# First batch of the first attention convolved, projected and split one learning step earlier; values cleared first

## Time and profile before

| | us |
|---|---|
| median of three runs | 3385.29 (3382.37 to 3389.59) |
| the profiled execution | 3388.66 |
| its span | 3386.8 |

### The profile page before, as it was taken

The page is one execution under the profiler, slowest core; times in us unless marked ns, Lnnn a source line. Parts: engine busy times, 40 slices in busy tenths (PEclk is TensorE's granted clock), DMA queues, the critical chain, the costliest instruction groups (busy, mean ns, idle before and its releaser), DMA issues. The chain is left out here.

```text
span 3386.8 us, 83147 instructions
## 1 busy us (share of the span) xinstructions
PE 3115.7 (92%) x33099; PEld 1852.8 (55%) x33099; DVE 2534.1 (75%) x5014; ACT 2057.6 (61%) x4153; POOL 877.2 (26%) x783
## 2 busy tenths in 40 slices
PE   6887799999999999999999999789999999999997
PEld 5776322222223677777777777545555554555554
DVE  5777788888887476677667766677887877778874
ACT  6775288888888443333434334247777666776776
POOL 3322311111111322342233224224342211111110
PEclk9998799999999999999999999889999999999999
DMA  4100122222221110010001101223333232222222
GB/s 142 36 20 4 54 80 83 78 81 84 81 75 53 34 30 30 23 33 29 29 23 33 35 23 30 49 77 95 90 93 81 79 98 86 80 78 80 84 61 67
DMA packets 234976, 204.91 MB, mean 61 GB/s; under 512 B 74340, under 2 KB 190852, under 8 KB 234500
## 3 DMA queue, kind: packets, MB, share of 16 engines
q1 hardware_dynamic: 228484, 195.50, 20.1%
q0 software_dynamic: 6144, 4.72, 1.0%
HBM read 73.61 MB, written 59.39 MB: 39 GB/s over the span
## 5 line engine op out<-in xcount | busy, mean ns | idle before, releaser
L1624 DVE TENSOR_REDUCE b_maxima<-psum 128x2 f32<-128x1024 f32 (+3 forms) x768 | 779.8, 1041 | 227.0 <-PE psum L1421 216.9
L1565 ACT ACTIVATE b_prob<-psum 128x512 f32<-128x512 f32 (+2 forms) x1536 | 725.5, 526 | 298.4 <-PE psum L1454 292.0
L1624 DVE TENSOR_REDUCE c_maxima<-psum 128x2 f32<-128x1024 f32 x512 | 592.5, 1213 | 58.1 <-PE psum L1415 57.3
L1565 ACT ACTIVATE c_prob<-psum 128x512 f32<-128x512 f32 x1024 | 547.2, 600 | 113.9 <-PE psum L1447 97.3
L2378 PEld LDWEIGHTS psum<-consts_layer,a_hid 128*128 128x128 f32 x4096 | 477.5, 192 | 53.8 <-issue 53.6
L2368 PE MATMUL psum<-a_x1t,consts_layer 128*128 128x512 f32 x1024 | 462.1, 595 | 20.8 <-ACT a_hid L2438 13.8
L2378 PE MATMUL psum<-consts_layer,a_hid 128*128 128x128 f32 x4096 | 479.0, 275 | 0.0
L2438 ACT ACTIVATE a_hid<-psum,consts_layer 128x512 f32<-128x512 f32 x512 | 347.0, 687 | 197.2 <-PE psum L2368 190.5
L1478 PE MATMUL psum<-b_prob,b_v 128*32 128x128 f32 (+3 forms) x5632 | 398.4, 371 | 15.9 <-ACT b_c L1572 15.4
L1447 PE MATMUL psum<-b_qa,b_ka 64*128 64x512 bf16 (+3 forms) x2048 | 344.2, 303 | 40.1 <-ACT b_prob L1565 26.0
L2605 DVE SCALAR_TENSOR_TENSOR a_acc<-psum,a_gprob,a_acc 128x128 f32<-128x128 f32 x512 | 143.7, 343 | 261.1 <-PE psum L2378 233.1
(11 more groups left out here) (407 smaller groups left out, 4200.7 us busy)
## 6 DMA issues: line engine op xcount, KB each, us to landing
b_qa<-b_part SPq DMA_DIRECT2D x192, 128.0 KB
b_context<-b_c SPq DMA_DIRECT2D x64, 256.0 KB, 2.1
c_qa<-c_part SPq DMA_DIRECT2D x96, 128.0 KB, 2.5
c_ka<-c_part SPq DMA_DIRECT2D x96, 128.0 KB, 2.6
b_ka<-b_part SPq DMA_DIRECT2D x96, 128.0 KB
c_context<-c_c SPq DMA_DIRECT2D x32, 256.0 KB, 2.1
b_scale<-b_inverse SPq DMA_DIRECT2D x64, 128.0 KB
b_unscaled<-b_context SPq DMA_DIRECT2D x64, 128.0 KB
```

Source lines behind the costliest of these rows:

```text
L1565: self.nc.scalar.activation(out, src, ACT.Exp, scale=SCALE).then_inc(self.s.free, 1)
L1624: self.nc.vector.reduce_max(out, src, X).then_inc(self.m.free, 1)
```

## The change

- The convolution of batch 0 and its copies move from step 6 (`NC - 2`) to step 5 (`NC - 3`), behind the norm; it waits for the last silu of chunk 7. `transpose_k(7)` waits for its copies.
- The projection and its copies move from step 7 to step 6, behind `transpose_k(7)` and a wait for both copies of `kt`.
- The four operations of the splits move from GpSimd in step 7 to VectorE: three ahead of the update of step 6 (`vector_parts`), the last at the start of step 7 (`vector_last`).
- GpSimd clears `qa` and `ka` at the start of step 6 and not behind its roots.
- In the setup of the first attention, the values' buffer is cleared before the row of ones is set.

```diff
-    def pool_parts(self, pool, rest):
+    def vector_parts(self, dve, rest):
         nc, qk, part = self.nc, self.qk, self.part
-        pool.wait_ge(self.qk_copied, 2)
-        nc.gpsimd.tensor_copy(part[0][:, :, :], qk[:, :, :]).then_inc(self.parted, 1)
...
+        dve.wait_ge(self.qk_copied, 2)
+        nc.vector.tensor_copy(part[0][:, :, :], qk[:, :, :]).then_inc(self.parted, 1)
+        dve.wait_ge(self.parted, 1)
+        nc.vector.tensor_tensor(rest, qk[:, :, :], part[0][:, :, :], ALU.subtract).then_inc(self.parted, 1)
+        dve.wait_ge(self.parted, 2)
+        nc.vector.tensor_copy(part[1][:, :, :], rest).then_inc(self.parted, 1)
+
+    def vector_last(self, dve, rest):
+        dve.wait_ge(self.parted, 3)
+        self.nc.vector.tensor_tensor(self.part[2][:, :, :], rest, self.part[1][:, :, :], ALU.subtract).then_inc(self.parted, 1)
...
@@ learn, tensor: transpose_k(n)
+                    if n == NC - 1:
+                        pe.wait_ge(head.xc_copied, 2)
@@ learn, tensor, step s
-                    if s == NC - 1:
+                    if s == NC - 2:
+                        pe.wait_ge(kt_copied.sem, kt_copied.at(NC - 1, 2))
                         head.tensor_projection(pe)
...
                     norm(s)
-                    if s == NC - 2:
-                        pe.wait_ge(kt_copied.sem, kt_copied.at(NC - 1, 2))
+                    if s == NC - 3:
+                        pe.wait_ge(silu_ready.sem, silu_ready.at(NC - 1, 4))
                         head.tensor_convolution(pe)
@@ learn, gpsimd, step s
                     pool.wait_ge(mem_ready.sem, mem_ready.at(s, 0))
+                    if s == NC - 2:
+                        pool.wait_ge(proj_ready.sem, proj_ready.at(NC - 1, 4))
+                        pool.wait_ge(prod_ready.sem, prod_ready.at(NC - 1, 1))
+                        pool.wait_ge(xt_stored.sem, xt_stored.at(NC, 0))
+                        head.pool_clear()
...
                         output_deviations(s, h)
-                    if s == NC - 2:
-                        pool.wait_ge(proj_ready.sem, proj_ready.at(NC - 1, 4))
-                        pool.wait_ge(prod_ready.sem, prod_ready.at(NC - 1, 1))
-                        pool.wait_ge(xt_stored.sem, xt_stored.at(NC, 0))
-                        head.pool_clear()
-                    if s == NC - 1:
-                        pool.wait_ge(kn_ready.sem, kn_ready.at(NC - 1, 1))
-                        head.pool_parts(pool, tk[:, :, :].rearrange("p (k t) d -> p k (t d)", k=2))
@@ learn, vector, step s
+                    if s == NC - 1:
+                        head.vector_last(dve, rest)
                     for h in range(2):
                         hidden(s, h)
...
+                    rest = tk[:, :, :].rearrange("p (k t) d -> p k (t d)", k=2)
+                    if s == NC - 2:
+                        head.vector_parts(dve, rest)
                     update(s)
@@ Attention.pool_setup
         nc = self.nc
+        if self.done:
+            self.pool_value(pool, 0)
         nc.gpsimd.memset(self.one[:, :], 1.0).then_inc(self.tables_ready, 1)
...
-        self.pool_value(pool, 0)
+        if not self.done:
+            self.pool_value(pool, 0)
```

## The result

The changed kernel takes 3391.07 us (median of 18 runs, 3385.84 to 3399.01); the kernel before, timed beside it, takes 3385.47 (18 runs, 3381.62 to 3390.71). The ratio is 1.0017, 95% interval 1.001 to 1.0025: 5.6 us slower, where 3382.3 was forecast. The profiled execution took 3389.57 us (span 3387.8) against 3388.66 (span 3386.8) before.

A forecast was written before the change was run, and what follows sets the result against it. No engine is full in a learning step, so it is a chain of waits. -3.7 - 1.8 + 2.5 = -3.0 us, applied to the median 3385.29, gave 3382.3 us; range 3377.0 to 3388.5, chance 0.82.

The forecast's parts named there:

- Added: three VectorE operations ...: 0: Before step 6's update: three moved splits, 2.7 us, fit in VectorE's 3.18 us idle wait, costing 0.
- the fourth operation's 0: Ahead of step 7's hidden part: the last split, 1.23 us, fits in VectorE's 2.03 us idle wait, costing 0.
- any stretch behind 360 us changes its length by more than 1 us: Behind the learning stage: a stated sign that the forecast is wrong.
- Step 7's gradient part, -3.7: First squaring of y to next root: without GpSimd's splits it takes 25.95 us instead of 29.67.
- Step 6's hidden part, -1.8: Root to first squaring of y: moved convolution keeps TensorE's clock high, second tanh at 280.1 instead of 282.01.
- Rival B: Step 6's clock fall was chance, so the filler saves nothing: -0.5, 3384.8 us; 0.15 together with D.
- D: Step 7: VectorE's chain did not set the step, another wait takes over: about -0.5; 0.15 together with Rival B.
- Step 7's hidden part, +2.5: Root to first squaring of y: without the filler TensorE's clock falls, 13.70 us instead of 11.17.
- The projection, 0: Step 6: the moved products and key copies fit in free time, copies ending 0.4 us before along_y: 0.
- bound of +1.5: Step 6's projection: most it could cost if its second product ended 1.9 us later at the lower clock.
- Values' clearing, 0: First attention's setup: earlier clearing frees VectorE's v copy at most 0.4 us sooner, followed by idle time: 0.
- Three splits before L1033: Step 6, VectorE's wait before the update: three splits take 2.7 us, with 0.5 us to spare.

The follow-up runs named there:

- after_gpsimd: Changed kernel with the four splits back on GpSimd in step 7, the other moves kept: 3393.58 us, ratio 1.0028; run again 3389.45, 1.0013.
- before_pad8: Kernel before with eight harmless one-column VectorE memsets in its wait of step 6: 3377.60 us, ratio 0.998.
- after_pad4_again: Changed kernel with four harmless one-column VectorE memsets in step 6, run once more on the second chip: 3372.10 us, ratio 0.9966.
- before_pad4: Kernel before with four harmless one-column VectorE memsets in step 6, on a chip where the kernel before took 3412.58: 3421.87 us, ratio 1.0024.
- before_pad6: Kernel before with six harmless one-column VectorE memsets in step 6: 3396.74 us, ratio 1.0042.
- before_pad7: Kernel before with seven harmless one-column VectorE memsets in step 6: 3379.89 us, ratio 0.9986.
- gpsimd_pad8: Changed kernel with the splits back on GpSimd, plus eight one-column VectorE memsets in step 6: 3383.69 us, ratio 0.9998.
- before_again: Kernel before, unedited, traced a second time: 3386.6 us (one run).
- before_values: Kernel before with only the values' clearing moved ahead of the row of ones: 3413.86 us, ratio 1.0, on the chip where the kernel before took 3412.58.

## Why the prediction was wrong

**The step that failed** is "Added: three VectorE operations ...: 0", with the fourth operation's 0, and the tacit 0 for everything behind 360 us. They cost nothing where they stand, as reckoned. But each added instruction also moves all later code of VectorE one place on, and the prediction priced instructions in time alone. Four places cost 1.47 us per iteration: over the five iterations between the rows 7.4 us, and about 1 more in the sixth. The sum of the profile closes: -7.0 at 410 us, +1.1 between 1070 us and the first jump, +7.4, +1.0, which is the lag of 2.5 at 2213 us; the rest of the kernel gives 1.5 back, and the spans differ by 1.0. The +1.1 arises between 1100 and 1130 us, where TensorE's clock is low for 10.2 us in the changed kernel and for 6.8 before; so it is in every kernel whose attention start is the short one (879.5 us from there to the first jump back, against 878.5). The text named the right alarm, "any stretch behind 360 us changes its length by more than 1 us", but gave it no mechanism and no chance.

**Step 7's gradient part, -3.7**: right. 25.66 us (324.14 to 349.80) against 29.67, so -4.0.

**Step 6's hidden part, -1.8**: the length was right, 11.91 us (273.41 to 285.32) against 11.9 forecast, and it is 11.9 in all seven profiles of kernels with the moved convolution. The gain was not right: it was luck of one profile. The fall of TensorE's clock at the end of step 5, taken as a rule from one execution, is none. In the seven profiles of kernels with the old learning stage, whose code is the same up to there, the hidden part takes 13.70, three times 12.46 and three times 10.78 us, on average 11.92, and step 6 takes 39.65, 38.36, 38.48, 38.20, 36.32, 36.32 and 36.31. So on average over these profiles moving the convolution gained nothing in this part. Rival B described this, and had 0.15 together with D.

**Step 7's hidden part, +2.5**: right in sign, +1.3 (12.46 us against 11.17), as the clock fell for half the time assumed (5.38 us for the product instead of 6.61). Six of the seven profiles with the moved convolution have 12.46; the fall was missing once, in after_gpsimd, with 10.77.

**The projection, 0**: wrong by 0.4. It ran at the lower clock (3.65 us, not 1.88; granted clock 0.69 from 289 to 292 us and 0.62 from 292 to 294), the key copy began at 293.83 and along_y follows it at 294.41, 9.09 us behind the first squaring and no longer 8.26: step 6's gradient part is 26.36, forecast 25.95. "I am wrong if along_y of step 6 waits for the key copy": it does, at this price, inside the bound of +1.5.

**Values' clearing, 0**: right. **Three splits before L1033**: right, 2.7 us and 0.59 to spare.

Sum of the learning stage: -4.1 measured in the two profiles, -3.0 forecast. Against the whole family of profiles it is less: steps 6 and 7 take 77.1 to 80.5 us with the old stage, on average 78.5 in seven, and 75.9 to 76.4 with the new, on average 76.2 in four, so the change is worth about 2.2 us there. Of the whole time, before_pad8 and after_pad4_again at the same place of the loop differ by 5.5 us in the median (3377.60 and 3372.10, from 11 and 5 executions that spread over 16.1 and 5.5 us). Their profiles differ by 3.2, of which 2.1 stood there already at root 5, behind the same code. So the gain of the change by itself is seen in both comparisons, and its size in the whole kernel is not settled.

**My theories on the way.** That the loop's place decides held in every kernel that tested it. Its shape I had not foreseen at first: dearer with each place up to the sixth, gone at the seventh. Several numbers on record for the pads missed by a little: before_pad4 came out 9.3 us above (5 to 9 expected), before_pad6 11.3 above (6 to 11), before_pad7 5.5 below (6 to 9), and gpsimd_pad8 11.6 above after_pad4_again (4 to 9). The expectation for after_gpsimd failed, as told: I had costed the splits on GpSimd by the earlier trace rows alone, in the place where they stood.

**Open.** Whether the attention's start takes 82.0 or 84.8 us goes with whether TensorE's clock falls twice, for 3.4 us each time, ahead of the long fall of 23.9 us that every trace has between 374 and 388 us (its start): it did in before, before_again, before_pad4, before_values and the three kernels with splits on GpSimd, and did not in pad6, pad7, pad8 and all with the splits on VectorE. The roots before it lie at different times in all of them; no run varied that alone. Places that leave between 8 and some 118 instructions of the target's block were not run either, so from how many on the second fetch is hidden stays open.

## What to carry to other kernels

Where a loop in hardware stands behind the edited code, an added or removed instruction is also a shift: compare the length of an iteration before and after, and the idle time put down to issue behind the jump, before judging the edit. The price is per jump, and here VectorE alone paid it, the one engine whose instructions were fetched again at each jump. Count the instruction packets behind a jump, with a few harmless instructions ahead of the loop and without: they find the cheap place. Here they were worth 19 us to the changed kernel, where the edit was forecast to bring 3. A fall of the clock read from one profile is a draw; a second profile of the kernel before would have shown that step 6's slow product was one (5.38 us instead of 6.61).

## What the runs showed of the hardware

- Behind each jump back a packet of 8192 bytes of instructions starts 1.0 to 1.3 us after the branch, and VectorE's next instruction 2.8 to 3.1 us after it. A second packet starts at 3.4 to 4.0 us. If seven instructions or fewer come before the second pause, the rest starts only 5.1 to 5.7 us after the branch: with seven left it costs 1.3 us per iteration, with three 2.8, with one 3.6, with none 0 (133.4, 134.9, 135.7 against 132.1).
- In the straight part of the loop's second pass the packets come 125 to 130 VectorE instructions apart (kernel before, 1327.91 to 1442.71 us).
- The later VectorE is at the jump, the more often TensorE's clock falls in the loop, each time to 1.2 GHz for 3.4 us: once with seven instructions left (five profiles), four and three times with three left (before_pad4, and the changed kernel at 1331.2, 1600.8 and 1870.5), five times with one left, never with none (six profiles). So the price of a place is in part VectorE's pause and in part the clock that follows it.
- The collision of GpSimd with VectorE goes one operation to one: four VectorE operations of 0.69 us took 1.41, 2.49, 1.52 and 2.60 beside GpSimd's 1.13, 2.44, 1.38 and 2.44.
- The same code up to the same point gives TensorE's hidden product 6.61, 5.38 or 3.69 us in different executions.
